# A routed MLP and a GRU in one kernel: odd tiles' down-projections and gate inputs 16 steps later, another end, first loads on two queues

## The chip, the cores and the metric

The kernel runs on one core of a Trainium2 chip. The metric is the device time of one execution in microseconds (us), as the median of several runs.

## The reference

```python
# layer 0, x: (8, 512, 256), t_emb: (8, 256)
shared = silu(xf @ w1) * (xf @ w3) @ w2                 # 512 hidden columns
s = sigmoid(concat([xf, tf]) @ router_W)                # 8 experts
_, topk_idx = top_k(s + router_bias, 2)
gates = s_sel / (s_sel.sum() + 1e-9)                    # combine: gates put at the 2 chosen experts
h = gelu(einsum('nc,ech->enh', xf, W1e)); y = einsum('enh,ehc->enc', h, W2e)
x1 = x + (shared + einsum('ne,enc->nc', combine, y)) / 3
# layer 1, a GRU over the 512 positions, h0 = cond
Z = sigmoid(xz + H @ Whz.T + bhz)                       # xz, xr, xh = x1 @ Wx*.T + bx*
R = sigmoid(xr + H @ Whr.T + bhr)
H_tilda = tanh(xh + R * H @ Whh.T + bhh)
H = Z * H + (1 - Z) * H_tilda;  Y = H @ Whq.T + bhq
return x1 + Y
```

Everything is fp32. All eight experts are computed for every token.

## The kernel before

**Tiles and steps.** A tile is 128 tokens: 16 positions (TS) of 8 sequences. There are 32 tiles, in 16 pairs; the GRU takes 512 steps, 16 per tile, each needing the state of the step before. While the GRU scans tile n, the layer-0 work of later tiles is put into the gaps of its steps. `place_of(n, s)` says for a step s of tile n which pair p of tiles the gap work is for and which step r of that pair's 32 (SPAN) it is:

```python
sp = s + TS * ((n + 1) % 2)
return (n + 1) // 2 + (sp >= FIRST_STEP), (sp - FIRST_STEP) % SPAN
```

All lists of the schedule are indexed by r. With FIRST_STEP = 6 the first step of an even tile n is r = 10 and the first of an odd tile r = 26; with 7 they are r = 9 and r = 25.

**A step.** TensorE: 16 small r products (L1129, `r_bank`), 16 z products, filler slot 1 (`fill_up`), 16 candidate products, filler slot 2 (`fill_rest`). ScalarE: tanh of r (`t_r`, L607), tanh of z (`t_z`, L609), `seed_r` (L548: copies the next step's gate inputs from `xs` into `r_bank`), `a_row` (L618), now and then `keep_states` or `score_tanh`, then `t_h` (L627), `seed_zc` (L556), then `consume_up` (tanh or gelu of an up-projection), `split_x` or a copy. VectorE: transpose of `t_r` (L881), `rhT` (L884), `factors` (L887), its slot 1 (one silu product of `shared_silu`, one operation of the routing, an x1 add), then `terms` (L896), transpose of `t_h` (L901), the two scans that give the new state `hist` (L904), then its slot 2 (`shared_hidden`, `accumulate`, `add_bias`, `finish_out`, `late_xT`, `split_x`). Each engine runs its instructions in exactly this order.

**Filler work per pair.** 12 units of up-projections (4 of the shared MLP, 8 experts), each 12 matmuls of 128x256 (`up`, L1008): 144 per pair, three to six in a step. For each tile 9 groups of down-projections g = 0 (shared, four chunks) to 8 (two chunks each), cut into halves of 128 columns (`down`, L981). Both tiles of a pair run together: three halves in slot 1 of r = 12 to 31 and four halves in slot 2 of three steps; group 8 follows at r = 0 (even tile) and r = 6 (odd). `accumulate(t, g)` adds a group's result times its gate into `x_all` (L764). Then `transpose_x1`, a copy to `x1T`, the projection to the gate inputs (PROJ1, four instructions' worth in slot 1), and `add_bias(t, q)` (L776) for each half q of the columns into `xproj`; its place is BIAS2. The output: `keep_states`, the product with Whq (OUT2), `finish_out`, `add_x1`, store.

**Gate inputs.** SP stores `xproj` to DRAM (`store_inputs`, after `xp_ready`) and reads it back in another layout into `xs` (`gate_rows`): four row DMAs for the first eight steps of a tile (counted in `xs_first`) and four for the last eight (`xs_second`). ScalarE waits for them, in order with its other work:

```python
if s + 1 == HALF:
    act.wait_ge(xs_second, 16 * NG * (n + 1))
if last:
    act.wait_ge(xs_first, 16 * NG * (n + 2))
seed_r(*after)
```

**Head.** Before the scan the kernel does all of pair 0: loads on SP's queue in the order x, w1, w3, We1, x, router, w2, We1, GRU weights, We2 (two DMAs), h0, six bias rows and the output bias, then blocks of x for tiles 4 and 5 (`load_late`), then the first `store_inputs`. Each weight of the up-projections is split into a high part (ScalarE) and a low part (VectorE). TensorE warms up with products of zeros (`warm`, L934), transposes x, then runs unit after unit; in round e (0 to 7) it runs the unit of expert e, down-projections of group e - 1 for tiles 0 and 1, and transposes of GRU weights. VectorE's `gate_biases` (L719) stands in round 4, waits for all bias rows and adds the two biases of each gate; `accumulate(0, 4)` comes behind it. After the last unit come group 8 of tile 0, 12 and then more up matmuls of pair 1, x1's transposes and the projections of tile 0, each full width (L1015), then the seeds of the first step.

**End.** After the last step: `keep_states`, the products with Whq, the bias add, the x1 add, one store of tile 31. Where no filler is left, `keep_busy` puts products of zeros into the slots.

## Time and profile before

| | us |
|---|---|
| median of 3 runs | 1298.71 (1296.39 to 1300.39) |
| profiled execution | 1297.89, its span 1296.1 |
| TensorE busy (PE) | 1265.9, 98% |
| VectorE busy (DVE) | 1005.8, 78% |
| ScalarE busy (ACT) | 799.3, 62% |
| GpSimd busy (POOL) | 6.8, 1% |

The span is the time from the first to the last instruction in the trace; all rows' times are counted from its start. The granted TensorE clock was 0.999 over the span. PE stands for matmuls, PEld for weight loads, SPq for SyncE's DMA queue.

### The profile page before, as it was taken

The page shows a single profiled execution, that of the slowest core. Times are in us where ns is not written, and L with a number is a line of the kernel's source. Part 1 is how long each engine was busy: PE and PEld are TensorE (multiplying, and loading weights), DVE is VectorE, ACT ScalarE, POOL GpSimd, SP SyncE. Part 2 cuts the span into 40 slices and gives each one's busy share as a digit, 9 for nine tenths or more (in the row PEclk, how much of TensorE's full clock was granted, in tenths as well). Part 3 has the DMA queues.
Part 4 walks back from the last instruction along what each step waited for, and adds up shares of the span by engine and source line. Part 5 has one row for each costly group of instructions (what it writes and reads, how often), then busy time and mean ns, then how long its engine had stood idle before and what let it go on. Part 6 is the DMA issues. An engine that isn't in the chain of part 4 may idle for free.

```text
span 1296.1 us, 84880 instructions
## 1 busy us (share of the span) xinstructions
PE 1265.9 (98%) x35818; PEld 877.3 (68%) x35818; DVE 1005.8 (78%) x6123; ACT 799.3 (62%) x4386; POOL 6.8 (1%) x26
## 2 busy tenths in 40 slices
PE   9999999999999999999999999999999999999886
PEld 8876776767667676766767677676766767676443
DVE  5578878787887878788787877878788787877665
ACT  4266666656666666666666666665666666666554
POOL 1000000000000000000000000000000000000000
PEclk9999999999999999999999999999999999999999
DMA  8201111111111111111110111111011110010100
GB/s 271 57 23 33 44 26 49 24 42 27 37 45 25 51 23 37 32 31 46 26 49 23 40 35 27 49 23 44 24 37 45 24 52 21 23 32 15 45 20 12
DMA packets 77748, 51.38 MB, mean 40 GB/s; under 512 B 43576, under 2 KB 74808, under 8 KB 77368
## 3 DMA queue, kind: packets, MB, share of 16 engines
q1 hardware_dynamic: 77368, 45.95, 14.0%
q8 instruction: 283, 4.64, 1.6%
q14 instruction: 97, 0.79, 0.2%
HBM read 29.13 MB, written 16.78 MB: 35 GB/s over the span
## 4 chain that ended last, share of the span: by engine, by line
PE 91%; DVE 5%; ACT 3%; issue 1%; DMA 0%; POOL 0%; SPq 0%; POOLq 0%; DVEq 0%
PE dn_ps L981 26%; PE up_ps L1008 25%; PE zc_bank L1129 20%; PE r_bank L1129 14%; PE aux L981 2%; DVE terms L901 2%; PE dn_ps L1015 1%; ACT t_r L607 1%; DVE hist L904 1%; ACT t_h L627 1%; DVE t_rT L881 1%; PE misc L981 1%; PE aux L934 1%; DVE gru_raw L725 0%; DVE factors L887 0%
## 5 line engine op out<-in xcount | busy, mean ns | idle before, releaser
L607 ACT ACTIVATE t_r<-r_bank 128x32 f32<-128x32 f32 x1024 | 146.2, 195 | 223.9 <-PE r_bank L1129 209.7
L881 DVE STREAM_TRANSPOSE t_rT<-t_r 128x32 f32<-128x32 f32 x1024 | 156.0, 191 | 154.2 <-ACT t_r L607 145.1
L627 ACT ACTIVATE t_h<-zc_bank 128x32 f32<-128x32 f32 x1024 | 146.0, 195 | 210.1 <-PE zc_bank L1129 210.0
L981 PE MATMUL dn_ps<-we_sb,hid_e 128*32 128x256 f32 (+1 forms) x4920 | 264.6, 333 | 0.6 <-issue 0.6
L1129 PEld LDWEIGHTS zc_bank<-whT,rhT 128*8 128x8 f32 x8192 | 118.5, 87 | 183.3 <-DVE rhT L884 180.3
L1129 PE MATMUL r_bank<-whT,hist 128*8 128x64 f32 x8192 | 210.5, 220 | 17.2 <-DVE hist L904 14.2
L1129 PE MATMUL zc_bank<-whT,rhT 128*8 128x64 f32 x8192 | 211.7, 220 | 4.4
L1129 PE MATMUL zc_bank<-whT,hist 128*8 128x64 f32 x8192 | 208.7, 219 | 0.0
L1129 PEld LDWEIGHTS r_bank<-whT,hist 128*8 128x8 f32 x8192 | 117.7, 88 | 122.1 <-DVE hist L904 99.4
L901 DVE STREAM_TRANSPOSE terms<-t_h 128x32 f32<-128x32 f32 x1024 | 156.8, 192 | 54.5 <-ACT t_h L627 18.8
L981 PEld LDWEIGHTS dn_ps<-we_sb,hid_e 128*32 128x32 f32 x4920 | 133.3, 110 | 31.4 <-issue 1.1
L556 ACT ACTIVATE zc_bank<-gru_raw 128x128 f32<-128x128 f32 x512 | 144.2, 282 | 16.0
L1008 PE MATMUL up_ps<-x_high,we_low 128*128 128x256 f32 x512 | 152.3, 297 | 0.0
L1008 PE MATMUL up_ps<-x_low,we_high 128*128 128x256 f32 x512 | 152.2, 297 | 0.0
L1008 PE MATMUL up_ps<-x_high,we_high 128*128 128x256 f32 x512 | 152.1, 297 | 0.2 <-issue 0.2
L904 DVE TENSOR_TENSOR_SCAN hist<-factors,terms 128x16 f32<-128x16 f32 x1024 | 145.5, 184 | 0.0
L1129 PEld LDWEIGHTS zc_bank<-whT,hist 128*8 128x8 f32 x8192 | 142.6, 90 | 0.0
L887 DVE STREAM_TRANSPOSE factors<-a_row 128x64 f32<-128x64 f32 x512 | 126.2, 246 | 19.4 <-ACT a_row L618 0.4
L884 DVE SCALAR_TENSOR_TENSOR rhT<-t_rT,hist 128x8 f32<-128x8 f32 x1024 | 133.4, 168 | 0.0
L764 DVE SCALAR_TENSOR_TENSOR x_all<-dn_ps,gates_all,x_all 128x256 f32<-128x256 f32 x256 | 119.3, 471 | 13.0 <-PE dn_ps L1015 8.4
L618 ACT ACTIVATE a_row<-t_z 128x64 f32<-128x64 f32 x512 | 125.7, 245 | 0.0
L548 ACT ACTIVATE r_bank<-gru_raw 128x64 f32<-128x64 f32 x512 | 114.3, 223 | 1.9 <-DMA gru_raw<-gate_inputs_by_group 1.6
(118 smaller groups left out, 1685.5 us busy)
## 6 DMA issues: line engine op xcount, KB each, us to landing
gate_inputs_by_group<-gru_raw SPq DMA_DIRECT2D x64, 192.0 KB, 2.0
gru_raw<-gate_inputs_by_group SPq DMA_DIRECT2D x256, 48.0 KB
xT_all<-in_x SPq DMA_DIRECT2D x448, 8.0 KB
x_all<-in_x SPq DMA_DIRECT2D x32, 128.0 KB
out<-gru_raw SPq DMA_DIRECT2D x32, 128.0 KB
x_all<-in_L_cond_W1e SPq DMA_DIRECT2D x1, 1536.0 KB, 10.8
we_sb<-in_L_cond_W2e SPq DMA_DIRECT2D x1, 1536.0 KB, 11.7
xT_all<-in_L_cond_w SPq DMA_DIRECT2D x2, 512.0 KB, 6.3
```

The lines of the kernel that those rows point to most:

```text
L556: act.activation(zc_bank[:, 0:2 * GW], xs[:, s, GW:RW], ACT.Copy).then_inc(seeded_zc, 1)
L607: act.activation(t_r[:, i, :], r_ps[:, i * Q:(i + 1) * Q], ACT.Tanh, scale=0.5).then_inc(tr_ready, 1)
L618: act.activation(a_row[:, :, :], t_z[:, :, :], ACT.Copy, bias=0.5, scale=-0.5).then_inc(a_ready, 1)
L627: act.activation(t_h[:, i, :], c_ps[:, i * Q:(i + 1) * Q], ACT.Tanh, scale=-1.0).then_inc(th_ready, 1)
L881: dve.transpose(t_rT[:, i, :], t_r[:, i, :]).then_inc(trT_done, 1)
L884: dve.scalar_tensor_tensor(rhT[:, i, :], t_rT[:, i, 0:B], 1.0, old[:, i, :], ALU.add, ALU.mult)\
L887: dve.transpose(factors[:, :, :, 1].rearrange("p i q -> p (i q)"), a_row[:, :, :].rearrange("p i q -> p (i q)"))\
L901: dve.transpose(terms[:, i, :, 0], t_h[:, i, :]).then_inc(thT_done, 1)
L904: dve.tensor_tensor_scan(hist[:, s, i, :, :].rearrange("p b e -> p (b e)"), factors[:, i, 0:B, :].rearrange("p b e -> p (b e)"), terms[:, ...
L981: done = pe.matmul(ps[Q * j:Q * (j + 1), col:col + cols], lhsT[:, Q * j:Q * (j + 1)], rhs, start=first, stop=last, tile_position=(0, Q * j ...
L1008: done = pe.matmul(up_ps[place % 2][:, half * PAIR:(half + 1) * PAIR], w, (x_low if low_x else x_high)[:, p % 2, :, k, :], start=(m % UP_M ...
L1129: done = pe.matmul(ps[Q * j:Q * j + B, :], lhsT[:, k, :], whT[:, gate, k, j * GW:(j + 1) * GW], start=False, stop=(k == NI - 1), tile_posi ...
```

## The change

Six parts.

1. The two tiles of a pair are no longer worked on together. The even tile's group 0 stands in r = 15 to 17 and its groups 1 to 7 in r = 22 to 31, three halves to a slot 1; group 8 follows at r = 0. The odd tile's come 16 steps later (r = 31 to 1, 6 to 15, 16). The four-half pieces in slot 2 are gone. Its transposes, projections (PROJ1 18 to 21) and bias adds (BIAS2 19 and 21) follow. FIRST_STEP becomes 7. Odd tiles' groups use other PSUM banks (`down_bank`), `hid_e` has a place for each of the 8 experts, and there are 8 steps with six up-projections in a pair's list where 11 were.
2. The routing of the next tiles starts later (BASE1 24, TANH1 25), with two of its operations in each of the steps 26 to 31.
3. The hidden product of the shared MLP stands in VectorE's slot 1 (HIDDEN1).
4. The head: x and w1 by halves on SP's queue while x of tile 1 and w3 are issued by ScalarE; x's high part is copied straight from the transposes in PSUM; We1 and We2 in four batches each; the down-projections of tile 1 for groups 1 to 8 leave the head.
5. The output bias is added with x1 (BIASED1) ahead of the product, and the copy of x1T always stands at ScalarE's end of a step.
6. The end: all positions but the last are kept early, the last by a small copy, and the last tile's output is made, added and stored in two halves.

```diff
-        FIRST_STEP = 6
+        FIRST_STEP = 7
...
-        PROJ1 = {2: (-2, 0, 0), 3: (-2, 0, 1), 4: (-2, 1, 0), 5: (-2, 1, 1), 8: (-1, 0, 0), 9: (-1, 0, 1), 10: (-1, 1, 0), 11: (-1, 1, 1)}
-        X1_2 = {1: -2, 7: -1}
-        OUT2 = {2: -4, 22: -3}
-        DOWN1 = range(12, SPAN)
-        DOWN2 = (15, 28, 31)
-        LAST_DOWN2 = {0: -2, 6: -1}
-        UP1 = [3 if r in (0, 1, 6, 7) else 0 for r in range(SPAN)]
-        UP2 = [0 if r in OUT2 or r in DOWN2 or r in LAST_DOWN2 else 3 if r in X1_2 else 6 if r in (8, 10, 13, 14, 16, 18, 19, 20, 23, 24, 25) else 5
-               for r in range(SPAN)]
-        GAP1, UP_GAP2, begin = [], [], 0
-        for r in range(SPAN):
-            middle = begin + UP1[r]
-            end = middle + UP2[r]
-            GAP1.append(range(begin, middle))
-            UP_GAP2.append(range(middle, end))
+        PROJ1 = {2: (-2, 0, 0), 3: (-2, 0, 1), 4: (-2, 1, 0), 5: (-2, 1, 1), 18: (-1, 0, 0), 19: (-1, 0, 1), 20: (-1, 1, 0), 21: (-1, 1, 1)}
+        X1_2 = {1: -2, 17: -1}
+        OUT2 = {2: -4, 18: -3}
+        LAST_DOWN2 = {0: -2, 16: -1}
+        UP_ORDER = [SPAN - 1] + [r for r in range(SPAN - 1) if r not in OUT2 and r not in LAST_DOWN2]
+        SIX_UPS = (4, 12, 14, 20, 22, 24, 26, 28)
+        UP_GAP2, begin = {}, 0
+        for r in UP_ORDER:
+            end = begin + (3 if r in X1_2 else 6 if r in SIX_UPS else 5)
+            UP_GAP2[r] = range(begin, end)
...
+        def place_downs(r, tile, halves):
+
+            for g, k in dict.fromkeys(half[:2] for half in halves):
+                taken = [half[2] for half in halves if half[:2] == (g, k)]
+                DOWNS1[r].append(("down", g, tile, k, taken[0], taken[-1] + 1))
+
+        for base, here in ((22, 0), (6, -1)):
+            for i in range(10):
+                place_downs(base + i, here, NEXT_HALVES[3 * i:3 * i + 3])
+        for early, here, later in ((15, 0, 0), (SPAN - 1, -1, 1)):
+            place_downs(early, later, FIRST_HALVES[0:2])
+            for i in range(2):
+                place_downs((early + 1 + i) % SPAN, here, FIRST_HALVES[3 * i + 2:3 * i + 5])
...
-        ADD2 = {0: [(NE, -2)], 6: [(NE, -1)], 14: [(0, 0)], 15: [(0, 1)], 17: [(1, 0)], 18: [(1, 1)], 19: [(2, 0)], 21: [(2, 1)], 23: [(3, 0)],
-                24: [(3, 1)], 25: [(4, 0)], 26: [(4, 1)], 27: [(5, 0)], 28: [(5, 1)], 29: [(6, 0)], 30: [(6, 1)], 31: [(7, 0), (7, 1)]}
-
...
-        UP_ACT2 = {3: 0, 6: 1, 8: 2, 10: 3, 13: 4, 15: 5, 18: 6, 20: 7, 23: 8, 25: 9, 27: 10, 31: 11}
-        X1_EVEN2, X1_ODD2 = 1, 7
-        SILU1 = {4: 0, 7: 1, 9: 2, 12: 3}
-        HIDDEN2 = {4: 0, 7: 1, 9: 2, 12: 3}
-        HEAD_UNITS = [u for r, u in SILU1.items() if r < FIRST_R]
-        BIAS2 = {3: (0, -2), 5: (1, -2), 10: (0, -1), 11: (1, -1)}
-        FINISH2 = {2: -4, 22: -3}
-        RESIDUAL1 = {3: -4, 23: -3}
-        X_HIGH2, X_LOW2 = 14, 16
-        LATE_XT2 = {8: 0, 13: 1}
-        LOGITS2 = {11: (0, 0), 12: (0, 1), 15: (1, 0), 17: (1, 1)}
-        BASE1, TANH1 = 18, 19
-        ROUTE_AHEAD1 = [r for r in range(20, SPAN) if r != 23]
-        ROUTE1 = [0, 1, 2, 5, 6, 8, 10, 11, 13, 14, 15, 16, 17]
+        ADD2 = {0: [(8, -2)], 1: [(0, -1)], 7: [(1, -1)], 8: [(2, -1)], 9: [(3, -1)], 11: [(4, -1)], 12: [(5, -1)], 13: [(6, -1)], 15: [(7, -1)],
+                16: [(8, -1)], 17: [(0, 0)], 23: [(1, 0)], 24: [(2, 0)], 25: [(3, 0)], 27: [(4, 0)], 28: [(5, 0)], 29: [(6, 0)], 31: [(7, 0)]}
+
+        UP_ACT2 = {3: 0, 6: 1, 8: 2, 10: 3, 13: 4, 15: 5, 20: 6, 22: 7, 24: 8, 26: 9, 28: 10, 31: 11}
+        SILU1 = {4: 0, 7: 1, 9: 2, 11: 3}
+        HIDDEN1 = {5: 0, 8: 1, 10: 2, 12: 3}
+        BIAS2 = {3: (0, -2), 5: (1, -2), 19: (0, -1), 21: (1, -1)}
+        FINISH2 = {2: -4, 18: -3}
+        BIASED1 = {3: -3, 19: -2}
+        LATE_XT2 = {14: 0, 20: 1}
+        X_HIGH2, X_LOW2 = 21, 22
+        LOGITS2 = {15: (0, 0), 19: (0, 1), 21: (1, 0), 23: (1, 1)}
+        BASE1, TANH1 = 24, 25
+        ROUTE_AHEAD1 = [r for r in range(26, SPAN) for _ in range(2)]
+        ROUTE1 = [0, 1, 2, 6, 13, 14, 15, 16, 17, 18, 20, 21]
...
         def turn(t, g):
-            return 2 * (NGR * (t // 2) + g) + t % 2
+            return NGR * t + g
+
+        def down_bank(g):
+            return dn_ps[0] if g % 2 == 1 or g == NE else dn_ps[1]
...
-            load_x(0, slice(0, 2))
-            sp.dma_start(w1_raw, w1.rearrange("(k p) h -> p k h", p=P)).then_inc(ld_w13[0], 16)
-            sp.dma_start(w3_raw, w3.rearrange("(k p) h -> p k h", p=P)).then_inc(ld_w13[1], 16)
-            sp.dma_start(we1_raw[:, 0:FEW], we1[0:FEW].rearrange("e (k p) h -> p e k h", p=P)).then_inc(ld_we1[0], 16)
+            load_x(0, slice(0, 1))
+            for half in range(2):
+                cols = w13_cols(half)
+                sp.dma_start(w1_raw[:, :, cols], w1[:, cols].rearrange("(k p) h -> p k h", p=P)).then_inc(ld_w13[half][0], 16)
+            def load_we1(i):
+
+                some = slice(FEW * i, FEW * (i + 1))
+                sp.dma_start(we1_raw[:, some], we1[some].rearrange("e (k p) h -> p e k h", p=P)).then_inc(ld_we1[i], 16)
+
+            def load_we2(i):
+
+                some = slice(FEW * i, FEW * (i + 1))
+                sp.dma_start(we2_sb[:, some], we2[some].rearrange("e (k p) c -> p e k c", p=P)).then_inc(ld_we2[i], 16)
+
+            load_we1(0)
...
+            load_we2(0)
+            load_we1(1)
             for r, _, _ in WEIGHTS:
                 load_gru(r)
-            sp.dma_start(we2_sb[:, 0:FEW], we2[0:FEW].rearrange("e (k p) c -> p e k c", p=P)).then_inc(ld_we2[0], 16)
-            sp.dma_start(we2_sb[:, FEW:], we2[FEW:].rearrange("e (k p) c -> p e k c", p=P)).then_inc(ld_we2[1], 16)
+            load_we2(1)
+            load_we1(2)
+            load_we1(3)
+            load_we2(2)
+            load_we2(3)
...
-                    if u >= HRING:
-                        act.wait_ge(dn_done, turn(2 * p + 1, u - HRING + 1) + 1)
-                    elif p > 0:
-                        act.wait_ge(dn_done, turn(2 * p - 1, (u - NE) % HRING + NE - HRING + 1) + 1)
-                    act.activation(hid_e[:, u % HRING, :, :].rearrange("p k t -> p (k t)"), ps[:, 0:2 * PAIR], ACT.Gelu)\
+                    if p > 0:
+                        act.wait_ge(dn_done, turn(2 * p - 1, u + 1) + 1)
+                    act.activation(hid_e[:, u, :, :].rearrange("p k t -> p (k t)"), ps[:, 0:2 * PAIR], ACT.Gelu)\
...
-                    act.wait_ge(tr_act, 1)
+                    act.wait_ge(tr_done, 1)
                 else:
                     act.wait_ge(tr_dve, 1)
                 act.activation(x_high[:, p % 2, :, :, :].rearrange("p n k t -> p (n k t)"),
-                               pair_xT(p), ACT.Copy).then_inc(x_high_ready, 1)
-
...
+            def keep_all_but_last():
+
+                act.wait_ge(hT_ready, NI * TS * NT)
+                act.wait_ge(y_done, NT - 1)
+                act.activation(yst_by_sequence[:, :, :, 0:TS - 1],
+                               hist[:, 0:TS - 1, :, :, 1].rearrange("p t i b -> p i b t"), ACT.Copy).then_inc(yst_ready, 1)
+
...
+            act.dma_start(x_all[:, 1, :], x[:, TS:2 * TS, :]).then_inc(ld_x[0], 16)
+            for half in range(2):
+                cols = w13_cols(half)
+                act.dma_start(w3_raw[:, :, cols], w3[:, cols].rearrange("(k p) h -> p k h", p=P)).then_inc(ld_w13[half][1], 16)
+            split_w13(0, 0)
+            split_x(0)
+            split_w13(0, 1)
+            split_w13(1, 0)
+            split_w13(1, 1)
+            consume_up(0, 0)
+            act.wait_ge(x_split, 1)
             take(0)
-            split_x(0)
...
-                dve.tensor_tensor(y_bias[:, :], aux[:, 0:C], bias_q[:, :], ALU.add).then_inc(y_bias_done, 1)
-
-            def add_x1(t):
-
-                dve.wait_ge(y_bias_done, t + 1)
+                dve.wait_ge(x1_biased, t + 1)
                 if t > 0:
                     dve.wait_ge(out_stored, 16 * t)
-                dve.tensor_tensor(y_out[:, :], y_bias[:, :], x_all[:, t, :], ALU.add).then_inc(y_ready, 1)
+                dve.tensor_tensor(y_out[:, :], aux[:, 0:C], x_of(t), ALU.add).then_inc(y_ready, 1)
+
+            def finish_last():
+
+                for i in range(NI):
+                    dve.wait_ge(hT_ready, NI * TS * NT + i + 1)
+                    dve.tensor_copy(yst_by_sequence[:, i, :, TS - 1], hist[:, TS - 1, i, :, 1]).then_inc(last_kept, 1)
+                dve.wait_ge(x1_biased, NT)
+                dve.wait_ge(out_stored, 16 * (NT - 1))
+                for h in range(2):
+                    cols = slice(h * P, (h + 1) * P)
+                    dve.wait_ge(y_done, NT + h)
+                    dve.tensor_tensor(y_out[:, cols], last_bank(h)[:, 0:P], x_of(NT - 1)[:, cols], ALU.add).then_inc(y_ready, 1)
...
+            dve.memset(zeros[:, :], 0.0).then_inc(zeros_ready, 1)
+            split_w13(0, 0)
             split_x(0)
-            split_w13()
+            split_w13(0, 1)
...
-                    if g == 0 and t > 1:
-                        pe.wait_ge(xp_ready, PIECES * (t - 1) + 1 - t % 2)
-                    if g == NE and t % 2 == 1:
-                        pe.wait_ge(xp_ready, PIECES * t)
-                    if g > 0 or t > 1:
-                        pe.wait_ge(acc_done, turn(t, g - 1) + 1)
+                    if g == 0 and t > 0:
+                        pe.wait_ge(acc_done, turn(t - 1, NE - 2) + 1)
+                    if g in (1, 2) and t > 0:
+                        pe.wait_ge(xp_ready, PIECES * (t - 1) + g)
+                    elif g == NE:
+                        pe.wait_ge(acc_done, turn(t, NE - 1) + 1)
+                    elif g >= 2:
+                        pe.wait_ge(acc_done, turn(t, g - 2) + 1)
                     if t == 0 and g == 0:
                         pe.wait_ge(ld_w2, 16)
-                    if t == 0 and g in (1, FEW + 1):
-                        pe.wait_ge(ld_we2[g > FEW], 16)
+                    if t == 0 and g > 0 and (g - 1) % FEW == 0:
+                        pe.wait_ge(ld_we2[(g - 1) // FEW], 16)
                     if g > 0 and t % 2 == 0:
...
-                    lhsT, w = hid_e[:, (g - 1) % HRING, k, cols], we2_sb[:, g - 1, k, :]
+                    lhsT, w = hid_e[:, g - 1, k, cols], we2_sb[:, g - 1, k, :]
...
+            def last_output():
+
+                pe.wait_ge(y_ready, NT - 1)
+                pe.wait_ge(yst_ready, NT)
+                for h in range(2):
+                    for i in range(NI):
+                        pe.wait_ge(last_kept, i + 1)
+                        done = product(last_bank(h), 0, P, yst[:, i, :], wqT[:, i, h * P:(h + 1) * P], i == 0, i == NI - 1)
+                    done.then_inc(y_done, 1)
+
...
-            warm(10)
...
+            warm(8)
+            pe.wait_ge(ident_ready, 1)
             transposes(0)
-            warm(16)
-            for place in range(NSH):
+            warm(4)
+            first_unit()
+            for place in range(1, NSH):
                 unit(0, place)
-                if place == 1:
-                    transposes(1)
-                    transposes(2)
+                if place < 3:
+                    transposes(place)
+            pe.wait_ge(consts_ready, 1)
             early_logits()
             m = len(HEAD_TR)
...
-                downs = [(e, 0)] if e < 2 else [(0, e - 1), (1, e - 1)]
+                downs = [(0, e)]
...
-            whole_down(0, NE - 1)
-            whole_down(1, NE - 1)
+            for k in range(NSH - 1):
+                down(1, 0, k, full=True)
             whole_down(0, NE)
+            down(1, 0, NSH - 1, full=True)
             for m in range(UP_MM // 2):
```

## Rows read from the trace of the kernel before

**Rows 1.** Chain of waits in the head: start, length, engine and line.
```profile
2.32 4.61 PE aux L934 x20
...
7.78 3.71 PE aux L934 x32
...
44.40 1.42 PE up_ps L1008 x12
45.82 4.32 PE dn_ps L1015 x20
...
51.86 2.67 PE dn_ps L1015 x8
...
55.14 1.98 DMA gate_inputs_by_group<-gru_raw
...
57.46 3.42 DMA gru_raw<-gate_inputs_by_group
```

**Rows 2.** SP's timeline, head: start, length, the issue of a DMA.
```profile
19.26 0.71 SPq L384 DMA_DIRECT2D we_sb<-in_L_cond_W2e  x1
...
32.08 0.50 SPq L393 DMA_DIRECT2D bias_q<-in_L_cond_bhq  x1
...
49.40 0.62 SPq L403 DMA_DIRECT2D x_all<-in_x  x1
```

**Rows 3.** DMA issues, first 62 us: size, us from issue to landing.
```profile
we_sb<-in_L_cond_W2e SPq DMA_DIRECT2D x1, 512.0 KB, 7.9
...
bias_q<-in_L_cond_bhq SPq DMA_DIRECT2D x1, 128.0 KB, 6.1
```

**Rows 4.** VectorE's timeline, rounds 4 and 5 of the head.
```profile
38.16 1.09 DVE L719 TENSOR_TENSOR bias_rows<-bias_rows,xT_all 128x256 f32<-128x256 f32 x3
...
40.44 0.48 DVE L764 SCALAR_TENSOR_TENSOR x_all<-dn_ps,gates_all,x_all 128x256 f32<-128x256 f32 x1
```

**Rows 5.** Timeline near the end, r products of two following steps.
```profile
1285.50 0.41 PE L1129 MATMUL r_bank<-whT,hist 128*8 128x64 f32 x16 [0.35 <-DVE hist L904]
...
1287.87 0.41 PE L1129 MATMUL r_bank<-whT,hist 128*8 128x64 f32 x16 [0.36 <-DVE hist L904]
```

**Rows 6.** Timeline, r products around a step with six ups.
```profile
137.69 0.41 PE L1129 MATMUL r_bank<-whT,hist 128*8 128x64 f32 x16
...
140.11 0.41 PE L1129 MATMUL r_bank<-whT,hist 128*8 128x64 f32 x16
```

**Rows 7.** VectorE's slot 1 in two steps: silu product, routing operation, terms, transpose.
```profile
143.90 0.38 DVE L725 SCALAR_TENSOR_TENSOR gru_raw<-gru_raw,up_ps 128x256 f32<-128x256 f32 x1
...
172.72 0.13 DVE L687 TENSOR_TENSOR hit<-sel,best 128x16 f32<-128x16 f32 x1
...
172.90 0.18 DVE L896 SCALAR_TENSOR_TENSOR terms<-factors,hist 128x16 f32<-128x16 f32 x1
...
173.19 0.31 DVE L901 STREAM_TRANSPOSE terms<-t_h 128x32 f32<-128x32 f32 x2
```

**Rows 8.** ScalarE's timeline: keep_states, t_h, and a score_tanh elsewhere.
```profile
138.81 0.63 ACT L563 ACTIVATE gru_raw<-hist 128x256 f32<-128x256 f32 x1
139.34 0.28 ACT L627 ACTIVATE t_h<-zc_bank 128x32 f32<-128x32 f32 x2
...
620.68 0.20 ACT L502 ACTIVATE score<-logits 128x16 f32<-128x16 f32 x1
```

**Rows 9.** Timeline: second bias add of a tile, next tile's first seed.
```profile
128.10 0.54 DVE L776 TENSOR_TENSOR gru_raw<-dn_ps,bias_rows 128x384 f32<-128x384 f32 x1
...
136.17 0.23 ACT L548 ACTIVATE r_bank<-gru_raw 128x64 f32<-128x64 f32 x1
```

**Rows 10.** Windows: stretch, length, busy by engine (PE, PEld, DVE, ACT, POOL), clock, DMA, GB/s.
```profile
132.60:133.10 0.50, 0.43 (x18) 0.23 (x21) 0.50 (x5) 0.47 (x2) 0.00 (x0) 1.00 0.35 98
```

**Rows 11.** Timeline at the end: the last scan, the last store's issue.
```profile
1290.00 0.28 DVE L904 TENSOR_TENSOR_SCAN hist<-factors,terms 128x16 f32<-128x16 f32 x2
...
1293.05 0.61 SPq L434 DMA_DIRECT2D out<-gru_raw  x1
```

More of the change, by code:

```diff
@@ L293, in in_slots @@
             return [(kind, i, tile, part, 0, 2) for part in range(count)]
[L295 removed]
+        FIRST_HALVES = [(0, k, h) for k in range(chunks_of(0)) for h in range(2)]
+        NEXT_HALVES = [(g, k, h) for g in range(1, NGR - 1) for k in range(chunks_of(g)) for h in range(2)]
         DOWNS1 = {r: [] for r in range(SPAN)}
         GAP2 = {r: [] for r in range(SPAN)}
[L298 to L306 removed]
+        def place_downs(r, tile, halves):
[9 more added lines that the diff above has]
+                place_downs((early + 1 + i) % SPAN, here, FIRST_HALVES[3 * i + 2:3 * i + 5])
         for r, tile in OUT2.items():
@@ L869, in late_routing @@
                     assert len(ops) == len(ROUTE_AHEAD1) + len(ROUTE1)
-                    ops[at]()
+                    for at, place in enumerate(places):
+                        if place == r:
+                            ops[before + at]()
             def body(n, scan, proj, outs):
@@ L1099, in fill_up @@
                     project(2 * p + tile, q, k)
-                elif 0 <= p < NPAIR:
-                    for m in GAP1[r]:
-                        up(p, m)
-                    for _, g, tile, k, begin, end in DOWNS1[r]:
-                        down(2 * p + tile, g, k, begin, end)
-                elif scan and p >= NPAIR:
-                    keep_busy()
+                else:
+                    downs = [(2 * p + tile, g, k, begin, end) for _, g, tile, k, begin, end in DOWNS1[r] if 0 <= 2 * p + tile < NT]
+                    for piece in downs:
+                        down(*piece)
+                    if scan and not downs:
+                        keep_busy()
             def fill_rest(p, r, scan):
@@ L1111, in fill_rest @@
                     transpose_x1(2 * p + X1_2[r])
-                if 0 <= p < NPAIR:
-                    for m in UP_GAP2[r]:
-                        up(p, m)
+                pair = p + 1 if r == UP_ORDER[0] else p
+                ups = UP_GAP2[r] if r in UP_GAP2 and 0 <= pair < NPAIR else ()
+                for m in ups:
+                    up(pair, m)
                 for kind, g, tile, part, begin, end in GAP2[r]:
@@ L1118, in fill_rest @@
                         down(t, g, part, begin, end)
-                    elif kind == "out" and 0 <= t < NT:
+                    elif kind == "out" and 0 <= t < NT - 1:
                         output(t, part)
-                if scan and p >= NPAIR and r not in LAST_DOWN2 and r not in OUT2:
+                if scan and r in UP_GAP2 and not ups:
                     keep_busy()
@@ L1179, in _ @@
                 up(1, m)
-            whole_down(1, NE)
             set_bits()
-            for m in range(2 * UP_MM, GAP1[FIRST_R].start):
+            for r in range(6, FIRST_R):
+                for _, g, tile, k, begin, end in DOWNS1[r]:
+                    down(2 + tile, g, k, begin, end, full=True)
+            for m in range(2 * UP_MM, UP_GAP2[FIRST_R].start):
                 up(1, m)
-                if m == 2 * UP_MM + 5:
-                    transpose_x1(1)
-            for r in range(FIRST_R):
-                if r in PROJ1 and PROJ1[r][0] == -1:
-                    project(1, *PROJ1[r][1:], full=True)
             def body(n, scan, proj, outs):
```

188 lines of the change are left out of this document (103 added, 85 removed).

## Prediction

> **What bounds the kernel now.** The rows of the chain of waits show a head in which TensorE works without a break from 2.3 us to 54.53 (51.86 plus 2.67, the projections of tile 0), then a stretch that only transfers fill: the second add of a bias, the store of the gate inputs from 55.14, the reload of the rows until 60.88 [rows 1]. There the scan begins. Its 512 steps are one serial chain through all engines. Where nothing but dummy products lie beside it, one r product starts 2.37 us after the other [rows 5]; a step with six up-projections takes 2.42 [rows 6]. So the span is a head of 61, steps at 2.375 plus small excesses, and a tail of some 6 us. TensorE is busy nearly all the time, but in a step with five up-projections it is not what ends the step. A gain has to come out of the head, the excesses or the tail; a loss comes from whatever is put into a gap of the chain that is already full.
>
> **Head, TensorE's work.** Tile 1's expert products for groups 1 to 7 leave the head. Twenty instructions, five groups, took 4.32 [rows 1], so a group is 0.865 and seven are 6.05. The first loads, the split from PSUM and the fewer warm products (12 for 26) let the first unit end earlier: warming began at 2.32 after GpSimd's constants and held TensorE until about 11.5 [rows 1]. I estimate unit 0 three us earlier. By this work alone the projections would end near 45.5.
>
> **Head, what stops it.** Two transfers don't move with it. First, gate_biases stands in VectorE's order of round 4 and waits for all bias rows; the last of them is issued at 32.08 and lands 6.1 later [rows 2, 3], at 38.2, just when gate_biases ran (38.16). Behind it stand the split of expert 7, the take and accumulate(0, 4), which ends at 40.92 [rows 4]. The same bytes lie ahead of these rows in the new order, so I leave 38.2. The new down(0, 6) waits for accumulate(0, 4). From 40.97 on TensorE has down(0, 6) 0.87, the last unit 1.42 [rows 1], down(0, 7) 0.87, three chunks of down(1, 0) 1.30, down(0, 8) 0.87, the fourth chunk 0.43, twelve ups 1.42, a transpose pair of about 0.3, the projections 2.67: 10.15, so they end at 51.1 and not at 54.53. Second, SP's queue is issuing tile 5's blocks until 50.02 [rows 2], and the first store stands behind them. It would be ready at about 50.4, so SP just lets it through; SP alone caps the gain at about 4.3. What follows is unchanged (6.35 from the projections to 60.88); TensorE has 5.8 of work left there (27 ups, the bits, nine half products) and is covered. Head: 3.4 less, between 1.5 and 4.4.
>
> The second queue adds nothing to this sum. The Trainium skill (DMA: Bandwidth & Descriptors, Issuing engines are not separate DMA queues) says that DMAs issued by different engines run on the same 16 DMA engines and save only issue time. No row here has two queues; by this rule the sum stays as it is, and if a second queue did bring the first units earlier, the wait for the bias rows would still swallow it.
>
> **Scan, fewer six-up steps.** The lists give 164 steps with six ups before and 119 after. 45 times 0.04 is 1.8 less. The downs lie three halves to a first slot in both; the second slots lose their four-half pieces. Neither costs.
>
> **Scan, two routing operations in one slot.** ROUTE_AHEAD1 puts two linked operations into steps 26 to 31. One starts at 172.72, terms follows at 172.90 and ends at 173.08, the transpose of t_h starts at 173.19 [rows 7]: 0.11 is free. A second operation with its wait is 0.18 more, so 0.07 shows. The nearest thing, a silu product of 0.38 in the same slot, fits [rows 7], so the bounds are 0 and 0.18; I take 0.06. Four steps with five ups, 14 pairs: 3.4; the two with six ups have 0.04 of it hidden: 0.6. Together 4.0 (0 to 15).
>
> **Scan, keep_states and score_tanh in one step.** TANH1 = 25 is the first step of odd n, where keep_states runs before t_h. keep_states starts at 138.81 and t_h at 139.34, with no idle time ahead of it [rows 8]. The tanh of 0.20 [rows 8] now stands between them: 0.11 by the pitch of such short operations (its bounds 0 and 0.20), 14 times: 1.5.
>
> **Scan, the hidden products move into the first slot.** They are of the silu product's shapes (0.38 fits with nothing to spare [rows 7]): 0 to 0.02 in three steps of 15 pairs, taken 0.5. The x1 bias takes the place of the x1 add. The copy of x1T goes to ScalarE's end of step, where odd tiles had it. Nothing for either.
>
> **Scan, the gate inputs arrive later.** This is the largest term. BIAS2 keeps rows 3 and 5 for even tiles and takes 19 and 21 for odd ones, while FIRST_STEP goes from 6 to 7: the second add of each tile now falls into step 12 of the 16 before it is needed; before it was 11 (even) and 1 (odd). Before, the add of an even tile ended at 128.64, and ScalarE wrote the next tile's first r seed at 136.17 [rows 9], 7.53 later, waiting for nothing. One step less leaves 5.1. The path between (store, wait, reload of four rows' DMAs) took 5.74 in the head, 55.14 to 60.88 [rows 1], with four more DMAs beside it. In the scan the last bytes of this reload move by 133.1 [rows 10], 4.5 after the add; the landing comes some time after the bytes. So it is late by 0 to 0.64; I take 0.3. The wait stands in ScalarE's order ahead of seed_r, and behind it are a_row, factors, terms, hist, all on the chain. In step 8 (odd n) the first slot holds a hidden product and no slack: 0.3, 15 times, 4.5. In step 24 the 0.11 is free and 0.04 hides under the sixth up: 0.15, 16 times, 2.4. Together 7.0 (0 to 16).
>
> Sum over the scan: -1.8 + 4.0 + 1.5 + 0.5 + 7.0 = +11.2.
>
> **Tail.** The last state is there at 1290.28 and the store issued at 1293.05 [rows 11], 2.77 later, after keep_states, sixteen products and two adds. Now only a small copy, a half product and one add stand before each half store; two halves overlap. I estimate the second store's issue 1.7 after the state: 1.05 less (0.5 to 1.5).
>
> Total: -3.4 + 11.2 - 1.05 = +6.75. The profiled execution took 1297.89 (span 1296.1 and 1.8 around it), so it would be 1304.6; the median of the three runs, 1298.71, stands 0.8 above it, so I forecast 1305.5.
>
> **Rivals.** (1) The rows arrive in time: if the reload ends within 5.1 us of the add, the 7.0 is gone: 1298.5, no change. For it: the bytes have moved after 4.5. Against it: 5.74 in the head. (2) The rows are late, but VectorE's and ScalarE's gaps take the additions: +6.75 - 6.0, 1299.5, no change. For it: the silu of 0.38 fits. (3) Faster: the reload needs less than 5.1 us and the gaps hold too, so that only head, tail and six-up steps count: -6.25, 1292.5. It decides from the point where the second routing operation fits in 0.11 us and the reload in 5.1. (4) The idle stretch in the head costs more than itself. ScalarE's split of expert 4, in round 1 and ahead of the gelu that down(0, 2) needs, now waits for the third we1 batch, which takes the place in the byte order of the batch that was issued at 19.26 and landed 7.9 later, at 27.2 [rows 2, 3]. TensorE would do almost nothing from 24 to 28.3. At the start its products took 0.23 us each (twenty in 4.61) and later 0.116 (thirty-two in 3.71), the lower and the full of its two levels (1.2 and 2.4 GHz) by duration, though it had been busy from 2.32 [rows 1]. Without that the unit of expert 6 would end at 40.0 by the pieces above, 1.0 before the bias limit. If the speed falls again in the gap, the next 2.7 us of work take twice as long, as the first ones did, and the projections end 1.7 later: 1307. The Trainium skill (TensorE: Matmul & The Clock Gate, Part 1: The HAM clock gate) says that an idle stretch can put the clock back to 1.2 GHz; by this rule the time is that 1307, and no row of the kernel before has such a gap. (5) The reload is late by the full 0.64: 31 times 0.34 more, 1316.
>
> **How the numbers follow.** A measurement of this kernel tells about 0.3% (3.9 us) from no change: the bounds are 1294.8 and 1302.6. The forecast has 0.45, rival 1 0.17, rival 2 0.15, rival 3 0.12, rival 4 0.08, rival 5 0.03. Slower: 0.45 + 0.08 + 0.03 and a part of rival 2, 0.60; same 0.28; faster 0.12. The range 1296 to 1312 leaves out rival 3 and rival 5. The forecast's own range is 1302 to 1310.
>
> **What would show it.** A wait of ScalarE's r_bank seed for the gate rows, some 31 times at about 0.3 us; r products 2.6 to 2.7 apart across each tile's last step; 2.43 in steps 27 and 29 to 31; the first r product at 57.8; gate_biases again at 38; a gap of TensorE at 25 to 28. It is wrong if no such wait shows, or if the scan starts much before 57.

## The result and the profile after

The changed kernel took 1308.82 us (median of 5 runs, 1304.88 to 1312.91), the kernel before 1299.09 in the same series (1296.39 to 1300.86). The ratio is 1.0072 with a 95% interval of 1.0057 to 1.0087, so it is slower by 7.4 to 11.3 us; the medians lie 9.7 apart. The forecast was 1305.5, 6.8 more than before, within 1296 to 1312. The profiled execution took 1304.88, its span is 1303.1; the forecast of a profiled execution was 1304.6. The total is near, but two groups of its terms were wrong by over 4 us each, in opposite directions.

**Scan.** I took the start of ScalarE's `t_z` in each of the 512 steps and sorted the 511 intervals by r. From the first to the last t_z the kernel before took 1226.7 us, the changed one 1236.25, 9.6 more. Here are some t_z of tile 5, from ScalarE's timeline of the changed kernel (start, length): the first three stand in r = 25, 26, 27, the next two in r = 29 and 30, the last two in r = 8 and the r = 9 that follows.

```profile
253.81 0.22 ACT L659 ACTIVATE t_z<-zc_bank 128x64 f32<-128x64 f32 x1
256.28 0.22 ACT L659 ACTIVATE t_z<-zc_bank 128x64 f32<-128x64 f32 x1
258.69 0.22 ACT L659 ACTIVATE t_z<-zc_bank 128x64 f32<-128x64 f32 x1
...
263.48 0.23 ACT L659 ACTIVATE t_z<-zc_bank 128x64 f32<-128x64 f32 x1
265.86 0.22 ACT L659 ACTIVATE t_z<-zc_bank 128x64 f32<-128x64 f32 x1
...
289.67 0.22 ACT L659 ACTIVATE t_z<-zc_bank 128x64 f32<-128x64 f32 x1
292.20 0.23 ACT L659 ACTIVATE t_z<-zc_bank 128x64 f32<-128x64 f32 x1
```

Step 25 (keep_states and score_tanh) takes 2.47. Step 26, with six ups and two routing operations, takes 2.41, and step 29, with two such operations and five ups, 2.38: nothing for the second operation. The length of an ordinary step is 2.38 with five ups and 2.42 with six. Step 8, the last of an odd tile, takes 2.53 here. Over all tiles the excess over the normal step is: step 8 6.6 us in 15 tiles (0.12 to 1.70 each), step 24 4.3 us in 16 tiles (below 0.15 in twelve, 0.70 to 1.79 in four), step 25 0.09 in each of 15. One of the four in step 24, 0.78 in tile 6, is no late row: the seed starts 0.20 after its t_z there, and what waits is a single product of TensorE, for nothing that the profile shows:

```profile
329.64 0.22 PE L1203 MATMUL zc_bank<-whT,rhT 128*8 128x64 f32 x1 [0.59 <-issue]
```

So the late rows themselves make 6.6 and 3.5.

What ends those waits stands in ScalarE's rows. This is the seed for tile 20, from its timeline (in brackets the idle time before, and its releaser):

```profile
834.00 0.22 ACT L659 ACTIVATE t_z<-zc_bank 128x64 f32<-128x64 f32 x1
834.84 0.23 ACT L583 ACTIVATE r_bank<-gru_raw 128x64 f32<-128x64 f32 x1 [0.61 <-DMA gru_raw<-gate_inputs_by_group]
```

In the next step, without a wait, the seed starts 0.13 after its t_z (837.12 and 837.25); here it starts 0.84 after. From the end of the tile's second bias add to this seed the kernel before had 7.5 us (even tiles, as in [rows 9]) and over 31 (odd tiles). Now it would be 5.1 without a wait. By the landings in the trace the path from add to landed rows took 5.14 to 7.20 us in the 31 tiles, 5.3 as the median, and over 6.1 in five of them (tiles 4, 9, 14, 15 and 19). In the kernel before the same path took 5.3 to 5.8 for even tiles, once 6.3, and 7.5 us of slack hid it. The changed kernel's longest is tile 19's. In the chain of waits, start and length, tile 18's store and reload come first, then tile 19's reload; the DMA rows give tile 18's store and tile 19's store with us to landing.

```profile
749.15 2.27 DMA gate_inputs_by_group<-gru_raw
...
751.74 2.74 DMA gru_raw<-gate_inputs_by_group
```

```profile
791.39 3.44 DMA gru_raw<-gate_inputs_by_group
```

```profile
gate_inputs_by_group<-gru_raw SPq DMA_DIRECT2D x1, 192.0 KB, 2.3
...
gate_inputs_by_group<-gru_raw SPq DMA_DIRECT2D x1, 192.0 KB, 3.4
```

The store took 1.1 us longer for tile 19 than for tile 18, and what follows it 0.7. The five long paths have one thing in common, which the DMA view shows by queue (packets, MB, share of the 16 engines' time). These are 0.7 us of tile 19's store, 788.1 to 788.8, and 0.7 of tile 18's, 749.6 to 750.3:

```profile
q1 hardware_dynamic: 88, 0.07, 28.0%
q8 instruction: 1, 0.02, 13.5%
...
q1 hardware_dynamic: 93, 0.07, 29.5%
```

Queue 1 carries the kernel's own store. Queue 8 carries packets of 16 KB of the kind "instruction", which no line of the kernel issues. In the changed kernel's trace such a packet starts 0.4 to 1.2 us after the add in these five paths and in no other. In all twelve traces (of the kernel before and run 2 the even tiles) it does so in 65 of 340 paths, and these took 5.8 to 7.6 us, 6.5 as the median, their stores 2.7 to 3.8; of the other 275, with a median of 5.3, nine took over 6. No run moves these packets, so that they lengthen the store is read from this agreement and not shown by a change.

The longest wait cost twice: the windows view (stretch, length, busy PE, PEld, DVE, ACT, POOL, clock, DMA, GB/s) shows TensorE empty and then at half clock.

```profile
795.00:796.00 1.00, 0.00 (x0) 0.00 (x0) 0.71 (x6) 0.97 (x6) 0.00 (x0) 1.00 0.59 111
...
797.00:798.00 1.00, 1.00 (x20) 0.53 (x16) 0.78 (x6) 1.00 (x5) 0.00 (x0) 0.50 0.19 20
798.00:799.00 1.00, 1.00 (x22) 0.79 (x11) 0.23 (x2) 0.43 (x3) 0.00 (x0) 0.50 0.19 34
799.00:800.00 1.00, 1.00 (x17) 0.78 (x19) 0.69 (x4) 0.14 (x1) 0.00 (x0) 0.50 0.03 3
```

After 1.72 us of idle TensorE the next step took 3.76, 1.3 above its 2.47. So the late rows cost 6.6 + 3.5 + 1.3 = 11.4 us in this execution, 7.5 of them in the five tiles with a long path. The scan's sum: 45 steps with five ups for six -1.8, step 25 +1.35, late rows +11.4, and 1.7 less of short stalls that fall anywhere (5.5 us in the trace before, 3.8 in this): 9.25 by the terms, 9.6 measured.

**Head.** The chain of waits of the changed kernel (to be read against [rows 1]):

```profile
18.45 8.61 DMA x_all<-in_L_cond_W1e
27.08 0.63 ACT we_high L575
27.71 0.49 ACT x_all L551
28.34 1.76 PE dn_ps L1075 x4
...
41.95 0.86 PE dn_ps L1075 x4
42.81 1.42 PE up_ps L1068 x12
44.23 3.45 PE dn_ps L1075 x16
...
49.32 1.34 PE dn_ps L1075 x4
...
51.27 3.08 DMA gate_inputs_by_group<-gru_raw
...
55.44 4.01 DMA gru_raw<-gate_inputs_by_group
```

VectorE's timeline, against [rows 4], and the windows of TensorE's gap:

```profile
38.89 1.10 DVE L771 TENSOR_TENSOR bias_rows<-bias_rows,xT_all 128x256 f32<-128x256 f32 x3 [1.26 <-DMA bias_q<-in_L_cond_bhq]
...
41.11 0.47 DVE L815 SCALAR_TENSOR_TENSOR x_all<-dn_ps,gates_all,x_all 128x256 f32<-128x256 f32 x1
...
51.97 0.56 DVE L826 TENSOR_TENSOR gru_raw<-dn_ps,bias_rows 128x384 f32<-128x384 f32 x1 [0.73 <-PE dn_ps L1075]
```

```profile
26.00:28.00 2.00, 0.00 (x0) 0.00 (x0) 1.36 (x3) 0.92 (x2) 1.36 (x3) 1.00 1.10 349
...
29.00:30.00 1.00, 1.00 (x4) 0.67 (x3) 1.00 (x3) 0.20 (x1) 0.00 (x0) 0.50 0.93 260
...
31.00:32.00 1.00, 1.00 (x6) 1.00 (x6) 0.00 (x0) 1.00 (x2) 0.00 (x0) 0.50 0.63 103
```

The gap of TensorE and the half clock of rival 4 are there (four down products 1.76 where others take 0.86). The third batch of We1 landed at 27.06; the prediction had 27.2. The projections' last add ended at 52.53, 2.6 earlier than before, and the first rows landed at 59.45, 6.9 later, where before they needed 5.8 (55.11 to 60.88). So the head is 1.4 shorter.

**End.** Against [rows 11]: VectorE's and SP's timeline.

```profile
1298.13 0.28 DVE L967 TENSOR_TENSOR_SCAN hist<-factors,terms 128x16 f32<-128x16 f32 x2
...
1299.79 1.25 SPq L472 DMA_DIRECT2D out<-gru_raw  x2
```

From the last state (1298.41) to the end of the span it is 4.7 us, before it was 5.8: 1.1 less. The second store is issued 2.0 after the last state, where 1.7 was expected and 2.77 measured before. In all -1.4 + 9.6 - 1.1 = +7.1, and the spans differ by 7.0.

### The profile page after: what moved, and what is told of

Same layout as the page of the kernel before. It is cut to its first block, busy times and chain, and to the rows that moved or that the text cites. A ratio compares the mean times of both kernels' runs of the same rounds, so it can differ in the third digit from the quotient of the medians.

```text
span 1303.1 us, 84974 instructions
## 1 busy us (share of the span) xinstructions
PE 1259.8 (97%) x35942; PEld 870.1 (67%) x35942; DVE 995.3 (76%) x6111; ACT 807.1 (62%) x4402; POOL 7.1 (1%) x25
## 4 chain that ended last, share of the span: by engine, by line
PE 80%; DMA 7%; DVE 6%; ACT 4%; SPq 2%; issue 1%
PE dn_ps L1041 23%; PE up_ps L1068 22%; PE zc_bank L1203 18%; PE r_bank L1203 13%; DMA gru_raw<-gate_inputs_by_group 4%; DMA gate_inputs_by_group<-gru_raw 3%; DVE terms L964 2%; PE aux L1041 2%; DVE hist L967 1%; ACT t_h L677 1%; ACT t_r L657 1%; PE dn_ps L1075 1%; PE misc L1041 1%; DMA x_all<-in_L_cond_W1e 1%; ACT a_row L668 1%
## 5 line engine op out<-in xcount | busy, mean ns | idle before, releaser
L1041 PE MATMUL dn_ps<-we_sb,x_all 128*32 128x256 f32 (+1 forms) x5160 | 276.6, 329 | 0.1
L1041 PEld LDWEIGHTS dn_ps<-we_sb,x_all 128*32 128x32 f32 x5160 | 138.7, 110 | 31.5 <-issue 0.6
L583 ACT ACTIVATE r_bank<-gru_raw 128x64 f32<-128x64 f32 x512 | 114.3, 223 | 12.1 <-DMA gru_raw<-gate_inputs_by_group 11.2
```

Source lines behind the costliest of these rows:

```text
L1041: done = pe.matmul(ps[Q * j:Q * (j + 1), col:col + cols], lhsT[:, Q * j:Q * (j + 1)], rhs, start=first, stop=last, tile_position=(0, Q * j ...
```

## The experiments

Three questions: whether the late rows are the loss and nothing else, what the additions to the steps cost, and what holds the head back. Run 3 and all from the fifth on are built on run 1.

**1. One step more for the gate inputs.**

```diff
-        FIRST_STEP = 7
+        FIRST_STEP = 6
...
                     accumulate(1, g)
+            shared_silu(1, 2)
```

(The scan then starts at r = 10 and not 9, so the silu product that stands in r = 9 has to be done in the head.)

> The changed kernel with FIRST_STEP = 6 again: every bias add stands one step (2.4 us) earlier against the step that needs it, all other lists unchanged. Theory (the rows of gate inputs arrive late): in the changed kernel the last step of a tile took 2.82 us on average in odd tiles and 2.69 in even ones, against 2.38 and 2.42 for such steps without a wait, 12.2 us in all with the slow TensorE that followed one long wait; the collision of keep_states and score_tanh (0.09 us, 15 times) goes too, since step 25 is then no tile's first. So no wait of the r seed for the gate rows, and 1304.9 less 12.2 and 1.4, about 1291.5 for the profiled run and 1291 to 1294 as the median. Rival (the additions to VectorE's and ScalarE's steps are what costs): a change of 1.4 at most, 1303 to 1308. Second rival (the transfers themselves have become longer in the new order, so one step more doesn't cure it): some waits of over 1 us stay, 1295 to 1300.

Measured: 1291.79 us (1289.36 to 1295.62, 7 runs), 0.9956 of the kernel before, interval 0.994 to 0.9973; its span 1289.1, 14.0 below that of the changed kernel, where 13.6 was expected. The tiles' last steps, now r = 9 and r = 25, take 2.38, none over 2.45; the page's row of the seed has 1.6 us of waiting, all of it at the first step:

```profile
L583 ACT ACTIVATE r_bank<-gru_raw 128x64 f32<-128x64 f32 x512 | 114.3, 223 | 1.7 <-DMA gru_raw<-gate_inputs_by_group 1.6
```

The changed kernel's page has 11.2 there. Both rivals are out: with 2.4 us more room nothing waits, and with the additions still there nothing is lost. The transfers didn't become shorter: six of the 31 paths took over 6.1 us here too, and tile 26's took 7.62, as long as the 7.5 of room. It landed 0.02 before its seed started.

**2. The late rows alone, in the kernel before.**

```diff
-        FIRST_STEP = 6
+        FIRST_STEP = 7
...
-            for u in HEAD_UNITS:
+            for u in (0, 1, 2):
```

(The loop in ScalarE's head, so that each unit is still consumed.)

> The kernel before with FIRST_STEP = 7 alone: only the even tiles' gate inputs come one step later against the scan (4 steps ahead of their need and not 5), odd tiles keep 15. Theory: 15 of 31 tile ends wait, each for 0.2 to 0.45 us on average with some long ones, 3 to 7 us in all: 1302 to 1306. Odd tiles show none. Rival (the wait is hidden by slack or belongs to the new order of the downs): the time of the kernel before, 1297 to 1300.

Measured: 1304.34 us (1302.68 to 1305.9, 6 runs), 1.0053 (1.0035 to 1.007). Only step 8 grew: four tiles of 15 took 3.54 to 3.95 and the others 2.41 to 2.59, 5.6 us above 2.415 in all. The other last step, 24, stayed at 2.42. So the cost follows the room for the transfer, without any of the new order, and it is made by few long transfers: 5.2 of the 5.6 come from four tiles, whose paths took 6.42 to 6.83 us.

**3. How many routing operations a step has room for.**

```diff
-        ROUTE_AHEAD1 = [r for r in range(26, SPAN) for _ in range(2)]
+        ROUTE_AHEAD1 = [26] + [27] * 2 + [29] * 3 + [30] * 4 + [31] * 2
```

> As the kernel with FIRST_STEP 6, with one linked routing operation in step 26, two in 27, none in 28, three in 29, four in 30 and two in 31 (instead of two in each of 26 to 31). The prediction held that a second operation shows 0.07 us; in the trace of the changed kernel such steps took 2.38 as others do. Theory (a slot of VectorE has room for two): steps 26, 27, 31 at 2.38 (2.42 where six ups stand), 29 at 2.38 to 2.5, 30 at 2.5 to 2.75, so 1 to 6 us more over 14 pairs than the kernel with FIRST_STEP 6. Rival (the room is that of any number, since ScalarE's t_h ends the gap later): 29 and 30 at 2.38 too.

Measured: 1301.16 us (one run). ScalarE's timeline, t_z of r = 27, 28, 29, 30 and 31 and the next:

```profile
255.65 0.23 ACT L659 ACTIVATE t_z<-zc_bank 128x64 f32<-128x64 f32 x1
258.03 0.22 ACT L659 ACTIVATE t_z<-zc_bank 128x64 f32<-128x64 f32 x1
260.45 0.22 ACT L659 ACTIVATE t_z<-zc_bank 128x64 f32<-128x64 f32 x1
263.02 0.22 ACT L659 ACTIVATE t_z<-zc_bank 128x64 f32<-128x64 f32 x1
265.80 0.23 ACT L659 ACTIVATE t_z<-zc_bank 128x64 f32<-128x64 f32 x1
268.18 0.22 ACT L659 ACTIVATE t_z<-zc_bank 128x64 f32<-128x64 f32 x1
```

Two operations: 2.38. Three: 2.57, four: 2.78, and so in all 14 pairs. The third costs 0.19 and the fourth 0.21; the second costs nothing. Steps 29 and 30 give 14 times 0.59, 8.3 us, of the 9.4 above run 1, more than the expected 1 to 6.

**4. score_tanh out of keep_states' way.**

```diff
-                    if EARLY <= 2 * p + 2 < NT and r == TANH1:
-                        score_tanh(p, slice(2 * p + 2, 2 * p + 4))
...
                         seed_zc(*after)
+                    if EARLY <= 2 * p + 2 < NT and r == TANH1:
+                        score_tanh(p, slice(2 * p + 2, 2 * p + 4))
```

> The changed kernel with score_tanh moved behind seed_zc in the same step 25, so that keep_states alone stands ahead of t_h. Theory: step 25 falls from 2.47 to 2.38 us, 15 times, 1.35 us; the steps 26 with the routing operation that needs the score don't grow. Rival (keep_states is what makes 2.47): step 25 stays at 2.47. The total varies by more than this with the late rows, so the step's length in the profile decides.

Measured: 1305.72 us (one run), no verdict by itself. Step 25 fell from 2.47 to 2.38, in 14 of 15 tiles; the collision cost 0.09. In this execution the late rows cost more than in the changed kernel's profile: 9.1 us in step 8 and 5.5 in step 24, with the same gap work and the same slack. Eight paths took over 6 us, the longest again tile 19's (7.32). TensorE was empty for 1.83 us there, and this time no half clock followed:

```profile
796.00:797.00 1.00, 0.00 (x0) 0.00 (x0) 0.12 (x1) 0.55 (x4) 0.00 (x0) 1.00 0.48 143
...
798.00:799.00 1.00, 1.00 (x52) 0.63 (x40) 0.68 (x6) 0.78 (x6) 0.00 (x0) 1.00 0.13 18
```

That is how far this cost moves between executions, and it fits that the changed kernel's five runs spread over 8.0 us and those before over 4.5.

**5 and 6. The head: blocks of x later; gelu ahead of the split.** Run 5 moves `load_late(EARLY + 1)` behind the first gate rows in SP's order. Run 6 has that too, and:

```diff
+                consume_up(0, NSH + e)
                 if e + 3 < NE:
                     split_we1(e + 3)
-                consume_up(0, NSH + e)
```

> The kernel with FIRST_STEP 6 (head up to the first r seed 59.0 us) with tile 5's blocks of x issued on SP's queue after the first gate rows and not before the first store. In the changed kernel the path from the last bias add of tile 0 to the first seed took 6.9 us where the kernel before needed 5.8 in its head and 5.3 in the scan; the adds came 2.6 us earlier than before. Theory (the blocks' 33 DMAs, issued until 50.6, still move while the store and the reload do): the path falls to 5.3 to 5.8, so the scan starts 1.1 to 1.6 earlier; the total 1290.2 to 1291. Rival (the path is long for another reason, a page or a bank of DRAM): 6.9 stays, and the head's length too.

> As the run before, and in ScalarE's head rounds the gelu stands ahead of split_we1(e + 3), so that group 2's down-projection no longer waits for the third batch of We1. Theory A (VectorE's gate_biases, which waits for the last bias row until 38.9, is as late as TensorE): the gap of TensorE at 25 to 28 shrinks below 1 us and its clock stays at full, but down(0, 6) waits for accumulate(0, 4), so only 0.3 to 0.5 us come out. Theory B (TensorE's gap and half clock are the only limit): 3 to 4.5 us earlier.

Measured: run 5 1289.42 us (0.9937, 0.9922 to 0.9952), run 6 1289.87 (0.9942, 0.9923 to 0.996). In run 5 the last add ended at 51.84 and the seed started at 57.83, 6.0 later and not 7.4 as in run 1 (51.68 to 59.03); the first r product moved from 59.31 to 58.11. TensorE has no idle time left there, so its own work is now the end of the head. Run 6 removed the gap (TensorE has no idle time over 0.25 us between 8.4 and 37.6) and gained little: the r product stands at 57.38. TensorE waits for accumulate(0, 4), and that for the bias rows. Its timeline:

```profile
35.20 1.03 PE L1076 MATMUL dn_ps<-we_sb,x_all 128*128 128x256 f32 x4
...
40.37 1.13 PE L1076 MATMUL dn_ps<-we_sb,x_all 128*128 128x256 f32 x4 [2.73 <-DVE x_all L815]
```

The 0.6 to 0.7 us that it gained is how much earlier the bias row landed in that execution (gate_biases at 37.63 and 38.24). Theory A.

**7, 9 and 10. The gap and its clock.** Each has run 5's edit and `gate_biases()` moved behind accumulate(0, 8). Run 9 has nothing more; 7 and 10 put products of zeros into TensorE's gap:

```diff
                 unit(0, NSH + e)
+                if e == 2:
+                    warm(24)      # run 10: 12
```

> FIRST_STEP 6, tile 5's blocks moved, gate_biases moved behind accumulate(0, 8) so that the bias rows bind nothing before the first add, and 24 products of zeros put behind the unit of expert 2, where TensorE waited 2.8 us for a gelu. The gap's end is not moved; what it does to the clock is. Theory (the fall of the granted clock to 0.50 for 3.4 us after the gap costs the head 1.7 to 1.9 us): no such fall, the projections 1.7 to 1.9 earlier than in the run with the blocks moved alone, less 0.3 to 1.1 for gate_biases, which now stands closer to the add: 0.8 to 1.6 in sum. Rival (the fall costs nothing, since something else bounds the head by then): 0 or a loss.

> FIRST_STEP 6, tile 5's blocks moved and gate_biases behind accumulate(0, 8); the gap of TensorE at 25 to 28 is left as it is. Theory (TensorE after its gap at half clock and the wait for the bias rows end at nearly the same time, within 0.5 us): moving gate_biases alone gives 0 to 0.5 in the time of the first r product against 58.1 with the blocks moved alone. Rival (the bias rows alone held the head back): 1.5 us or more.

> As the run with the gap filled, with 12 products of zeros (2.7 us by 0.223 each) and not 24 (5.4 us, which ran 2.5 us past the gap's end). Theory: no fall of the clock, the same 19.1 us from the first instruction behind the gap to the projections that it took there (21.0 with the fall), so the first r product 1.6 to 2.0 earlier than in the run that leaves the gap, about 56 to 56.5. Rival (what the gap ends with, a landing of We1, moves the later units too): less than 1.

Measured: run 7 1292.24 us (0.9956, 0.994 to 0.9972), run 9 1289.07 (0.9942, 0.9925 to 0.9959), run 10 1288.63 (0.9934, 0.9918 to 0.9951). Run 7 overfilled: 24 products took 5.4 us and the next down product began at 30.50, over two us late; the 24 were too many. But what follows ran at full clock: from that product to the projections 19.1 us. In the changed kernel (28.34 to 49.16) it took 20.8, without idle time. So the half clock costs 1.7. In run 9 the gap was shorter and no half clock followed it. It was shorter because a half clock had come earlier, from 14.0 to 17.4, behind an empty stretch of 2.31 us, so that TensorE reached the gap 1.0 later (26.50 for 25.52); run 5's head is the same in this, with the half clock from 14.2 on and a gap of 1.47. Run 9's rows:

```profile
28.02 1.10 PE L1075 MATMUL dn_ps<-we_sb,x_all 128*128 128x256 f32 x4 [1.52 <-ACT x_all L551]
...
47.17 2.77 PE L1075 MATMUL dn_ps<-wxT,x1T 128*128 128x384 f32 x8
```

28.02 to 47.17 is again 19.15, and so is run 10's 27.33 to 46.48. Run 9's r product came at 56.71, 1.4 before run 5's, which also had full clock and where TensorE waited for accumulate(0, 4): the bias rows held run 5 back (28.26 to 48.47 took 20.2 there, 1.1 more than 19.15; the rest is a gap that ended 0.24 earlier and a path 0.1 shorter), against what I expected. Run 10 gained 0.7 more (55.99), all of it from a gelu that came 0.7 earlier in that execution, so it says nothing about the clock. The medians of runs 5, 9 and 10 lie within each other's intervals.

**8. All three edits of the head.**

> FIRST_STEP 6 with all three edits of the head: blocks of x moved, gelu ahead of the split, gate_biases behind accumulate(0, 8). Theory: with the bias rows out of the way the time that TensorE gains (gap of 2.8 less about 1, half clock 1.8) comes out: the first seed 3 to 4 us before that of the run with the blocks moved alone, the total 1286 to 1288. Rival (the fourth batches of We1 and We2 bound the last units then): 1 to 2 us.

Measured: 1286.66 us (1285.63 to 1288.49), 0.9915 (0.9895 to 0.9935): the fastest kernel by its median, 11 us under the 1297.81 of the kernel before in its series. The first r product stands at 55.85, 2.3 before run 5's, less than the expected 3 to 4: TensorE's work is without a break from 29.9 on, also behind the projections, and the seed (55.57) waited only 0.17 for the rows.

## Why the prediction was right, and where it was not

**Late gate inputs: right mechanism, size wrong.** The step "5.1 us of room against a path of up to 5.74, so late by 0 to 0.64, I take 0.3" gave 7.0; 11.4 was measured. The usual lateness was near the forecast: the median path is 5.3, 0.2 over the room, and the 26 tiles with such paths cost 3.9 together. The term failed in taking one lateness for all tiles, from one path in the head and one window. The landings spread from 5.14 to 7.20, five of them over 6, and these five cost 7.5, with the half clock that followed one of them. The trace before held a path of 6.3 that its slack had hidden; the prediction didn't look for the longest of 31. Runs 1 and 2 show the mechanism in both directions.

**Two routing operations: wrong.** "0.11 is free, a second operation is 0.18 more, so 0.07 shows" gave 4.0; nothing was there. VectorE's timeline of step 29 of tile 3:

```profile
186.02 0.13 DVE L742 TENSOR_TENSOR mask<-hit,best 128x16 f32<-128x16 f32 x1
186.19 0.17 DVE L747 SCALAR_TENSOR_TENSOR sel<-mask,sel 128x16 f32<-128x16 f32 x1
186.39 0.18 DVE L959 SCALAR_TENSOR_TENSOR terms<-factors,hist 128x16 f32<-128x16 f32 x1
186.49 0.30 DVE L964 STREAM_TRANSPOSE terms<-t_h 128x32 f32<-128x32 f32 x2
```

The transpose starts 0.10 after terms, before the 0.18 of terms are over; in [rows 7] it starts 0.29 after. So the room was 0.29 less 0.10, 0.19, and one more operation at a pitch of 0.17 to 0.20 just fits. I had taken a row's length for the time until the next can start. Run 3 confirms it: room for two, and the third costs a full 0.19. Rival 2's argument, "the silu of 0.38 fits", was the better row, since two operations at that pitch are no longer than it. The 0.5 for the hidden products was nothing in three of their four steps: without late rows, in run 1, steps 5, 10 and 12 take 2.38, 2.38 and 2.42, as others do, and step 8 takes 2.40. So rival 2 was true in most of its 6.0, but rows later than it allowed made up for that.

**keep_states and score_tanh: right.** 0.11 was forecast and 0.09 measured, and run 4 removes it.

**Six-up steps and end: right.** -1.8, with 2.38 and 2.42 as forecast; -1.1 for -1.05, though 0.8 of it is the earlier issue, where 1.05 was forecast, and the rest came behind it.

**Head: 2.0 short, by two steps of the sum.** -3.4 was forecast and -1.4 came, the first r product at 59.75 and not at 57.8. The bias rows landed 0.7 later than assumed. TensorE, after its gap and half clock, began down(0, 6) at 41.95, 0.4 after accumulate(0, 4) had ended (41.58). So the bias rows nearly bound it but didn't: TensorE's own work did. By these two the projections ended 0.85 later than forecast. The path from the adds to the rows was 1.15 longer, since tile 5's blocks of x were issued until just before and still moved; "what follows is unchanged" was the step that failed there, and run 5 shows it. Rival 4 saw the half clock. It gave it 2.7, of which 1.0 would be hidden by the bias rows; it was 1.7, and since the bias rows bind nearly as late, 0.4 of it shows. The Trainium skill (TensorE: Matmul & The Clock Gate, Part 1: The HAM clock gate) says that an idle stretch can bring the clock back to 1.2 GHz. The traces agree that it can, and show that it need not: 0.50 after 2.8 us without work in the head and after 1.7 in the scan, but 1.00 after 2.5 us in the same head (10.76 to 13.31), after run 4's 1.83 and after run 6's 2.73 (37.65 to 40.37):

```profile
38.00:40.00 2.00, 0.00 (x0) 0.00 (x0) 2.00 (x6) 0.80 (x2) 0.09 (x1) 1.00 0.12 17
41.00:42.00 1.00, 1.00 (x9) 0.95 (x8) 1.00 (x3) 0.00 (x0) 0.00 (x0) 1.00 0.23 65
```

The second queue was not run alone, so what it does by itself stays open.

So the direction was right for the reason given, and the size was right by luck: 4.5 of operations that cost next to nothing and 1.7 fewer short stalls on one side, 4.4 more of late rows and 2.0 less from the head on the other. The median lies 4 above the profiled execution. Whether that is late rows again, no profile of those four runs shows; run 4's profile makes it likely.

## What to carry to other kernels

When a transfer's slack is cut to about its usual length, its cost is set by the longest landings, not by the median: read every occurrence in the trace, look at what else moved during the long ones (here packets that no line of the kernel issues), and keep room for the worst. For work put into a slot between two waits, take the time between starts, not the lengths of the rows, as the room, and the longest thing that already fits there as a bound. Where two limits end at nearly the same time, as the bias rows and TensorE here, taking one away shows little of what both are worth: against run 5 the gelu order alone gave 0.7, late biases alone 1.4, both 2.3.
